# First attention's maximum in two reductions, the head product in one bank, the experts' gathers ahead of their scatters

## The reference

```
x = x + xattn0(ctx, layernorm(x), mask)      # 4 heads of 64, keys: 77 context rows + 1024 rows of x
x = x + ffn0(layernorm(x))                   # 256 -> 1024 -> 256, gelu, a per-batch low rank term
x = x + xattn1(layernorm(x), ctx)            # 8 heads of 64, keys: 77 context rows
x = x + ffn1(layernorm(x))                   # 8 experts; each takes its 257 best rows of a batch
# xattn0, per head: softmax(rmsnorm(q) rmsnorm(k)^T / 8, masked) v, then out @ Wo^T + bo
# ffn1: out.at[b_idx, sel_idx].add(gated)
```

## Time and profile before

| | us |
|---|---|
| median of three runs (lowest, highest) | 900.57 (897.47, 904.03) |
| the profiled execution: time, span | 895.13, 893.3 |
| PE busy, share of the span | 769.3, 86% |
| DVE busy | 545.1, 61% |
| ACT, POOL busy | 397.8, 331.4 |
| first attention's units | about 65 to 383 |
| experts | about 665 to 893 |

### The profile page before, as it was taken

The page is one execution under the profiler, slowest core; times in us unless marked ns, Lnnn a source line. Parts: engine busy times, 40 slices in busy tenths (PEclk is TensorE's granted clock), DMA queues, the critical chain, the costliest instruction groups (busy, mean ns, idle before and its releaser), DMA issues.

```text
span 893.3 us, 12574 instructions
## 1 busy us (share of the span) xinstructions
PE 769.3 (86%) x4724; PEld 613.5 (69%) x4724; DVE 545.1 (61%) x1132; ACT 397.8 (45%) x721; POOL 331.4 (37%) x303
## 2 busy tenths in 40 slices
PE   2659988989999999989998989887139999899996
PEld 2546554765555545567968979886139999899996
DVE  6556776566577576255552459895847566575542
ACT  2434543445345334455272234343016656466462
POOL 6403001210020011126362123333425788787863
PEclk9959999999999999999999999997559999999999
DMA  6000000000000010010002020112200544235422
GB/s 176 1 0 1 1 1 1 1 1 0 1 1 1 1 49 1 1 47 3 2 0 90 1 95 1 48 48 95 95 24 25 142 132 129 74 93 142 136 32 24
DMA packets 20110, 38.38 MB, mean 43 GB/s; under 512 B 4507, under 2 KB 15633, under 8 KB 17745
## 3 DMA queue, kind: packets, MB, share of 16 engines
q1 hardware_dynamic: 13393, 29.14, 9.7%
q0 software_dynamic: 6656, 8.43, 5.4%
HBM read 29.02 MB, written 8.40 MB: 42 GB/s over the span
## 4 chain that ended last, share of the span: by engine, by line
PE 63%; DVE 22%; issue 6%; ACT 6%; POOL 2%; DMA 1%; another core or an unknown queue 0%; SPq 0%; ACTq 0%; DVEq 0%; POOLq 0%
PE ps L443 19%; PE ps L1058 10%; PE ps L581 9%; PE ps L681 5%; DVE mx L1224 4%; PE ps L545 3%; PE ps L598 3%; PE ps L599 2%; DVE qkn L1182 2%; PE ps L522 2%; DVE rep L1611 1%; DVE sm L1423 1%; ACT htmp L1918 1%; PE ps L995 1%; DVE Pb L1427 1%
## 5 line engine op out<-in xcount | busy, mean ns | idle before, releaser
L581 PE MATMUL ps<-PT,VA 128*65 128x512 f32 (+1 forms) x288 | 147.2, 593 | 0.2 <-ACT PT L1860 0.2
L1058 PE MATMUL ps<-he,wh 128*128 128x258 f32 x768 | 105.6, 291 | 0.0
L1860 ACT ACTIVATE PT<-ps 128x512 f32<-128x512 f32 x128 | 76.0, 594 | 65.7 <-PE ps L599 65.1
L1224 DVE TENSOR_REDUCE mx<-ps 128x1 f32<-128x1104 f32 x64 | 83.5, 1305 | 33.1 <-PE ps L545 32.7
L443 PE MATMUL ps<-GT,wh 128*128 128x258 f32 x768 | 97.7, 287 | 1.1 <-DVE GT L1700 1.1
L1058 PEld LDWEIGHTS ps<-he,wh 128*128 128x128 f32 x768 | 96.9, 192 | 0.4
L443 PEld LDWEIGHTS ps<-GT,wh 128*128 128x128 f32 x768 | 94.5, 191 | 1.5 <-issue 1.5
L1730 DVE TENSOR_TENSOR he<-het,he 128x516 fp32r<-128x516 f32 x64 | 44.7, 699 | 58.1 <-ACT he L1754 39.9
L2188 POOL TENSOR_TENSOR rs<-rs,half 128x4 f32<-128x4 f32 (+2 forms) x19 | 18.2, 957 | 162.5 <-DVE rs L1098 132.8
L2197 POOL TENSOR_TENSOR ssq<-ssq,half 128x4 f32<-128x4 f32 x32 | 32.5, 1017 | 118.4 <-DVE ssq L1170 118.2
L2446 POOL DMA_INDIRECT out_dram<-ye,idx x40 | 62.4, 1560 | 24.7 <-DVE ye L1712 15.1
(11 more groups left out here) (262 smaller groups left out, 1520.1 us busy)
## 6 DMA issues: line engine op xcount, KB each, us to landing
wr<-in_w1e_dram SPq DMA_DIRECT2D x8, 1024.0 KB
wr<-in_w2e_dram SPq DMA_DIRECT2D x8, 1024.0 KB
x<-in_x_dram SPq DMA_DIRECT2D x4, 512.0 KB, 6.8
w<-in_w_dram SPq DMA_DIRECT2D x2, 1024.0 KB, 4.7
y_dram<-yr SPq DMA_DIRECT2D x3, 512.0 KB, 3.0
out_dram<-x SPq DMA_DIRECT2D x3, 512.0 KB, 4.1
gt<-y_dram,idx POOLq DMA_INDIRECT x40
out_dram<-ye,idx POOLq DMA_INDIRECT x40
```

Source lines behind the costliest of these rows:

```text
L581: pe.matmul(bank[6 + hf][0:65, :], VA[b][0:K, kt, h, :], PT[u % 4][0:K, :], start=kt == 0, stop=kt == 8).then_inc(p_pv, 1)
L1058: op = pe.matmul(bank[dc][:, 0:258], w2h[i][:, wc_], he[j][:, m, 258 * c:258 * c + 258], start=n == 0, stop=n == 23)
L1224: v.tensor_reduce(mx[:, hi % 2, qt:qt + 1], ps[:, 0:3, 0:368], AX.XY, ALU.max).then_inc(v_mx, 1)
L1860: a.activation(PT[u % 4][0:K, :], bank[4 + u % 2][0:K, :], ACT.Exp, bias=0.0 if K == 128 else mcol[:, b:b + 1]).then_inc(a_exp, 1)
```

## The change

The maximum of a tile is read in two instructions. TensorE multiplies into bank 2 first and signals p_m3, then into banks 0 and 1 and signals p_mx; each bank is cleared just ahead of its own matmul. DVE reduces bank 2 (368 columns) behind p_m3 and frees it with v_m3, then banks 0 and 1 (736 columns) behind p_mx, which v_mx frees. Both results go to a new tile mxp. After every fourth query tile a third reduction over mxp (128x4 out of 128x4x2) writes mx and signals v_mr, for which max_row waits now. wo_tile uses bank 2 always, but for head 7. On GpSimd gather(ex + 2) stands ahead of all five scatters of expert ex.

```diff
@@ tensor_program @@
             def max_tile(hi, qt):
                 h = hi % H0
-                for j in range(3):
-                    clear(j)
                 if qt == 0:
                     pe.wait_ge(v_ka, 2 * hi + 2)
-                for j in range(3):
+
+                for j in (2, 0, 1):
+                    clear(j)
                     op = pe.matmul(ps[:, j, 0:368], QA[:, h, 128 * qt:128 * qt + 128], KA[:, h, 368 * j:368 * j + 368],
                                    start=True, stop=True)
-                    busy[j] = (v_mx, 8 * hi + qt + 1)
+                    busy[j] = (v_mx if j < 2 else v_m3, 8 * hi + qt + 1)
+                    if j == 2:
+                        op.then_inc(p_m3, 1)
                 op.then_inc(p_mx, 1)
 
             def max_row(hi, hf):
                 clear(0)
-                pe.wait_ge(v_mx, 8 * hi + 4 * hf + 4)
+                pe.wait_ge(v_mr, 2 * hi + hf + 1)
@@
             def wo_tile(hi, qt):
-                h, m = hi % H0, qt % 3
+                h, m = hi % H0, 2 if hi < 7 else qt % 3
@@ vector_program @@
             def max_tile(hi, qt):
+                if qt % 4 == 0 and hi:
+                    v.wait_ge(v_mr, 2 * (hi - 1) + qt // 4 + 1)
+                v.wait_ge(p_m3, 8 * hi + qt + 1)
+                v.tensor_reduce(mxp[:, qt, 1:2], ps[:, 2:3, 0:368], AX.XY, ALU.max).then_inc(v_m3, 1)
                 v.wait_ge(p_mx, 8 * hi + qt + 1)
-                if hi >= 2 and qt % 4 == 0:
-                    v.wait_ge(p_mT, 2 * (hi - 2) + qt // 4 + 1)
-                v.tensor_reduce(mx[:, hi % 2, qt:qt + 1], ps[:, 0:3, 0:368], AX.XY, ALU.max).then_inc(v_mx, 1)
+                v.tensor_reduce(mxp[:, qt, 0:1], ps[:, 0:2, 0:368], AX.XY, ALU.max).then_inc(v_mx, 1)
+                if qt % 4 == 3:
+                    v.wait_ge(v_mx, 8 * hi + qt + 1)
+                    v.wait_ge(v_m3, 8 * hi + qt + 1)
+                    if hi >= 2:
+                        v.wait_ge(p_mT, 2 * (hi - 2) + qt // 4 + 1)
+                    v.tensor_reduce(mx[:, hi % 2, qt - 3:qt + 1], mxp[:, qt - 3:qt + 1, :], AX.X, ALU.max).then_inc(v_mr, 1)
@@ gpsimd_program, per expert @@
-                for k in range(3):
-                    scatter(ex, k)
                 if ex + 2 < NE:
+
                     g_.wait_ge(p_gT, 4 * ex + 4)
                     gather(ex + 2)
-                for k in range(3, 5):
+                for k in range(5):
                     scatter(ex, k)
```

More of the change, by code:

```diff
@@ L158, in build @@
         mx = RA("mx", [128, 2, 8])
+        mxp = RA("mxp", [128, 8, 2])
         mrt = [[RA(f"mrt{i}{j}", [4, 128], F32R) for j in range(2)] for i in range(2)]
@@ L323, in build @@
         p_mx = sem("p_mx")
+        p_m3 = sem("p_m3")
         p_mT = sem("p_mT")
@@ L360, in build @@
         v_mx = sem("v_mx")
+        v_m3 = sem("v_m3")
+        v_mr = sem("v_mr")
         v_x = sem("v_x")
@@ L1220, in max_tile @@
             def max_tile(hi, qt):
+                if qt % 4 == 0 and hi:
+                    v.wait_ge(v_mr, 2 * (hi - 1) + qt // 4 + 1)
+                v.wait_ge(p_m3, 8 * hi + qt + 1)
+                v.tensor_reduce(mxp[:, qt, 1:2], ps[:, 2:3, 0:368], AX.XY, ALU.max).then_inc(v_m3, 1)
                 v.wait_ge(p_mx, 8 * hi + qt + 1)
-                if hi >= 2 and qt % 4 == 0:
-                    v.wait_ge(p_mT, 2 * (hi - 2) + qt // 4 + 1)
-                v.tensor_reduce(mx[:, hi % 2, qt:qt + 1], ps[:, 0:3, 0:368], AX.XY, ALU.max).then_inc(v_mx, 1)
+                v.tensor_reduce(mxp[:, qt, 0:1], ps[:, 0:2, 0:368], AX.XY, ALU.max).then_inc(v_mx, 1)
[5 more added lines that the diff above has]
+                    v.tensor_reduce(mx[:, hi % 2, qt - 3:qt + 1], mxp[:, qt - 3:qt + 1, :], AX.X, ALU.max).then_inc(v_mr, 1)
             def wo_tile(hi, qt):
-                b, m = hi // H0, qt % 3
+                b, m = hi // H0, 2 if hi < 7 else qt % 3
                 v.wait_ge(p_wo, 8 * hi + qt + 1)
```

## The result

The kernel after takes 894.11 us (median of 20 runs, 887.89 to 899.34), the kernel before 902.26 in the runs beside it (20 runs, 896.07 to 911.53). The ratio is 0.992, with 0.990 to 0.994 as its 95% interval. Of 902.26 us that is 7.1 us less (the two medians lie 8.2 apart). The forecast was 894.0, from 6.6 us less.

A forecast was written before the change was run, and what follows sets the result against it. PE was taken to bound the kernel, busy 86% of the span, with output products held by the maximum. Terms -7.5 + 2.4 - 1.5 + 0 = -6.6 us on the 900.57 median gave 894.0 us, range 888 to 902.

The forecast's parts named there:

- The held products: First attention, heads 1 to 7: output products held by the maximum in 22 of 56 cases start earlier; -7.5 us.
- the whole maximum ends at 308.0 instead of 308.13: Pair in head 5: where DVE is early, splitting the reduction costs nothing and ends the maximum even 0.1 us earlier.
- Two reductions and a third, +2.4: First attention: 15.6 us of new DVE work, mostly taken by idle time, costs 2.4 us; bounds 0 and 15.6.
- My sign of being wrong: First attention: DVE holding PE between 100 and 200 us by more than 3 us over before.
- Ahead of head 0, -1.5: Before head 0's first scores: PE's open waits for the maximum shrink; -1.5 us, bounds 0 and 3.6 us of idle time.
- The gathers, 0: Experts: gathers start 5.2 us sooner, but nothing close waits for them or the scatters; 0 us, bounds -7.1 and +1.8.
- L995's third group as late as before: Experts: the transposes' third group, late five times for 7.1 us in all, stays late, since DVE's subtraction ends its wait.
- The bound of -7.1: Experts: the gain in us if the lateness of L995's third group came from the gather transfers after all.
- The rival built on it: Experts: earlier rows let the five late groups through, -7.1 us on top of the forecast, 887 us; chance 0.05.
- The whole relief: First attention: DVE's idle time takes all its new work and the struck stalls go too, -10.4 us, 890.2; chance 0.20.
- VectorE as the bound: Heads 0 to 4: new Vector work delays what PE waits for, mean +2.9 us, 903.5; chance 0.11.
- The stall renamed: First attention: pairs are held by x in bank 2 instead; only 1 to 3 us gained, 898.5 us; chance 0.14.

The follow-up runs named there:

- the split alone: Attention part with the maximum in two parts, but the output product in the bank of its tile's number, against the kernel before: 883.58 us, ratio 0.995.
- the doubled part: Attention part of the change with the reduction of the maximum's first part done twice, against the kernel before: 898.91 us, ratio 1.012.
- the third group: Four kernels run on one chip beside the kernel before, which took 888.49 us there.
- the bank alone: Kernel before with the output product of heads 0 to 6 always in bank 2, maximum still read in one part: 890.64 us, ratio 1.002.
- the gathers alone: Kernel before with only the new order of gathers, ahead of the scatters: 915.36 us, ratio 1.020.
- the attention alone: Kernel after with the old order of gathers, between the scatters, against the kernel before: 890.22 us, ratio 0.991.

## Why the prediction was right

**The held products.** The stalls went as forecast. Read from the starts as before, 22 products were held for 7.5 us, and one is now, at 264.5 us, for 0.7 (0.8 forecast, of the 1.45 of the earlier trace rows). Pairs take 3.52 us against 3.51 forecast. The attribution was wrong. The step "the whole maximum ends at 308.0 instead of 308.13" was mis-sized: the split alone shows 307.86. I had added a gap of 0.04 us between two reductions, and they overlap by 0.08; and the first starts on bank 2 while the other two are being filled. So the split would have freed 13 of the 22 products, and about half of the 7.5 us, without the move to bank 2. The move alone brings nothing (274.7 against 274.5). On top of the split it takes the held products from 3.9 us to 0.7, but the matmuls that wait for x go from 2.5 us in 3 places to 4.6 in 11, and the trace gains 1.3 us.

**Two reductions and a third, +2.4.** As far as it can be estimated, the size came out by two errors that cancel, which is luck. The pair costs 0.54 + 0.91 - 0.08 = 1.37 us where the one took 1.31, and DVE's busy time rises by 4.9 us in the attention (4.1 over the span) and not by some 15. (The section of the Trainium skill that I had weighed, VectorE: DVE Perf Modes, "The DRAIN you can't avoid", also says that an operation which nothing holds starts earlier; the 0.08 us agrees with that.) But a microsecond of it costs more than I took: I had 2.4 for 15.6, 0.15 each (the 0.24 of the expectation puts it on the two parts alone), and the doubled part shows 0.48, an upper value, since it also holds back the second part. 4.1 to 4.9 us at 0.48 is 2.0 to 2.4, an estimate. What PE waits for now is of that size: starts of the maximum held by x (L1246) went from 2.7 us in 3 places to 4.6 in 11, and the idle time of the transposes behind yb (L456, L452 before) from 1.2 us to 2.4. My sign of being wrong didn't come: between 100 and 200 us PE's idle time behind DVE is 6.8 us, and 7.0 before. (DVE waits for L545 ahead of 43 of the 64 maxima in the trace, and not 39 as the prediction counts.)

**Ahead of head 0, -1.5.** Measured 65.04 - 63.94 = 1.1, and 61.36 where I had about 61.

**The sum in the attention.** -7.5 + 2.4 - 1.5 = -6.6 stands against -5.9 after and -8.2 in the kernel without the gather of 2 rows, whose attention is the same code. The two differ by the stretch of 6.8 us at half clock at 150 us. Two windows show it, after and without the gather of 2 rows, columns as in the earlier trace rows:

```profile
150.00:157.00 7.00, 7.00 (x16) 3.67 (x17) 2.88 (x6) 1.84 (x4) 1.40 (x2) 0.51 0.00 1
```

```profile
150.00:157.00 7.00, 6.04 (x28) 3.66 (x27) 4.03 (x10) 2.88 (x7) 2.21 (x3) 1.00 0.00 1
```

The profiled execution of the kernel before, from which the prediction's rows come, hasn't the stretch either, so -8.2 is the one to compare. The attention gained 1.6 us more than forecast: 7.4 from head 1 on instead of 5.1, and 0.8 to 1.1 ahead of it instead of 1.5. The waits named here don't account for all of these 2.3 us; where the rest came from is open.

**The gathers, 0.** The number held: 0.992 with them and 0.991 without, in intervals of 0.2 to 0.4%. The argument didn't. "L995's third group as late as before" is false (7.1 us went to 1.1), and the sign that I had named as a refutation, the experts' time changing by more than 2 us, came: 227.5 became 230.6. 2.3 of these 3.1 us are in expert 0, which takes 30.3 us with either order and 28.0 before. The stretch at half clock reaches 5.5 us into it instead of 3.0, and its seventh activation `het` starts 3.7 us behind the sixth instead of 2.2. In experts 1 to 7 the order itself makes 1.1 us (200.3 against 199.2). The late activation moved from steps 6 and 7 of an expert to steps 3 to 5, and so the wait moved from L995 to L447. I had put the lateness down to "ACT's late copy" and asked no further what made ACT late. The bound of -7.1, that the lateness comes from these transfers, was right about the cause: without them, or with plain copies, 10 us of the experts go. The rival built on it was wrong that the new order would bring them.

**The base.** The three runs gave 900.57; beside the kernel after it was 902.26. The ratio forecast was 0.9927, and measured 0.992. That the two agree within 1 us is partly luck: the attention gained more than the sum had, and the experts, put at 0, took some of it back. The interval of 0.990 to 0.994, some 4 us wide, couldn't tell these parts apart.

**The rivals.** The whole relief (890.2) would have needed DVE's new work free; PE's longer waits for x and yb speak against it. VectorE as the bound didn't come; even the doubled part, with 31.7 us more of its work, cost half of that. The stall renamed is there for 1.9 us of 7.5, and the split alone, which has no more waits for x than before, shows that it came with the move to bank 2.

## What to carry over

When an engine waits for a reduction over several buffers, split it and fill first the buffer that is read first: reading the first part while the rest is filled was worth 6.1 us here, and which buffer the waiting work goes to 1.3. Before comparing two traces by a few us, look whether both have the same stretches at half clock; one of them was worth 2.1 us here. Price new work on a second engine by doubling it, since its cost per microsecond (0.48 here) isn't its share of busy time. Before moving DMAs in a GpSimd queue, ask not only who waits for them but what GpSimd computes next and what VectorE does beside it: here moving them alone cost 2%, two thirds of it by that.

## What the runs showed of the hardware

- Activations of ScalarE start up to 2.9 us late in the experts, by nothing that the trace records, where gathers of 128 rows and one of 2 rows are issued by GpSimd together. Leaving out either kind, or plain copies in their place, ends what PE feels of it: experts 1 to 7 take 189.8 to 189.9 us instead of 199.2 to 200.3. On the chip of the third group none is late, though the kernel with the bank alone has the experts of before unchanged. Whether 16 rows instead of 2 cure it wasn't decided, and why chips differ stays open.
- VectorE's bf16 product of 128x240 took 0.40 us ahead of GpSimd's subtractions. Where it began beside the first of five it ended 0.25 to 0.28 us behind that one and so took 0.45 to 2.38 us, mostly 1.50. In four experts of the kernel with the gathers alone it ended 0.27 or 0.28 us behind the fifth and took 6.8 to 6.9. There the first subtraction had followed a DMA without idle time, and the first two overlapped by 0.48 us instead of 0.03. Why this happens when the gathers are moved alone and not together with the attention is open. The Trainium skill (Trainium Architecture — The Big Picture, "What this means for kernel authors") has VectorE and GpSimd exclude each other at a port by a lock, not by sharing it; the ends 0.25 to 0.28 us behind a subtraction fit. Why the product gets in behind the first of five or only behind the last, no run here shows.
- The stretches of granted half clock differ between executions of the same code, and with them the times: the 6.8 us near 150 us cost 2.1 us, with the attention of before (276.6 against 274.5) as after (269.2 against 267.1). Of the attention alone, 883.25 us came with a mean clock of 0.947 and 894.29 with 0.938.
